# Expert tiles: turning the hidden activations in 32x32 blocks on VectorE and placing them with ScalarE, in place of TensorE's transposes

## The reference, cut to what matters

```python
top_v, top_i = jax.lax.top_k(x @ gate_w, 2)
top_p = jax.nn.softmax(top_v, axis=-1)
combine = zeros((T, 8)).at[arange(T)[:, None], top_i].add(top_p)
g = einsum('th,ehi->tei', x, Wg)           # 256 -> 704
u = einsum('th,ehi->tei', x, Wu)           # 256 -> 704
d = einsum('tei,eih->teh', silu(g) * u, Wd)  # 704 -> 256
expert_out = einsum('te,teh->th', combine, d)
shared = silu(x @ Sg) * (x @ Su) @ Sd
```

## Time and profile before

| what | value |
|---|---|
| median of 3 runs | 1810.65 us (1805.61 to 1811.26) |
| the profiled execution, its time | 1814.42 us |
| the profiled execution, its span | 1812.6 us |
| busy: PE, DVE, ACT, POOL | 1569.5, 1152.0, 854.1, 1046.7 us |
| expert stage, first gate multiplication to last down multiplication | 1183.86 to 1770.90 us |
| granted TensorE clock over the span | 0.945 |

### The profile page before, as it was taken

How to read it: one execution, slowest core, us unless ns; L and a number is a source line. 1 busy time by engine, 2 the same in 40 slices (tenths; PEclk the granted TensorE clock), 3 DMA queues, 4 the chain that set the end, 5 groups by cost and what they waited for, 6 DMA issues and landing times.

```text
span 1812.6 us, 23920 instructions
## 1 busy us (share of the span) xinstructions
PE 1569.5 (87%) x7068; PEld 1057.0 (58%) x7068; DVE 1152.0 (64%) x1928; ACT 854.1 (47%) x1480; POOL 1046.7 (58%) x1233
## 2 busy tenths in 40 slices
PE   5888798898898898898898768699999999999990
PEld 2354555555555655655555645467777777777770
DVE  2299998898898898898898997222222222222225
ACT  3566657657658657658657554222112222121214
POOL 0579779779778779778778885312222222222224
PEclk9899899999999999999999968799999999999995
DMA  3111112211211111111111652514212222222216
GB/s 96 48 35 48 47 47 73 73 48 49 73 45 55 65 46 58 65 42 58 60 48 47 219 157 73 171 42 113 43 33 34 33 33 34 34 34 34 34 28 191
DMA packets 84393, 116.21 MB, mean 64 GB/s; under 512 B 11120, under 2 KB 58576, under 8 KB 84272
## 3 DMA queue, kind: packets, MB, share of 16 engines
q1 hardware_dynamic: 63344, 82.94, 14.6%
q0 software_dynamic: 16704, 27.57, 7.8%
q10 hardware_dynamic: 4224, 4.19, 0.7%
HBM read 81.05 MB, written 33.10 MB: 63 GB/s over the span
## 4 chain that ended last, share of the span: by engine, by line
PE 37%; DVE 5%; issue 4%; POOL 3%; ACT 2%; DMA 1%; DVEq 0%; POOLq 0%; ACTq 0%; SPq 0%
PE A L1255 10%; PE bA L1214 9%; PE bH L1214 9%; DVE arena L862 2%; PE bY L1238 2%; POOL arena L1019 1%; PE bH L592 1%; DVE arena_t L879 1%; DMA sum_scratch<-arena_t 1%; PE A L1246 1%; PE A L522 1%; PE A L1238 1%; PE A L577 1%; PE A L564 1%; PE A L555 1%
## 5 line engine op out<-in xcount | busy, mean ns | idle before, releaser
L1019 POOL TENSOR_TENSOR arena<-arena 128x512 f32<-128x512 f32 x512 | 645.5, 1273 | 175.5 <-DVE arena L862 173.0
L736 ACT ACTIVATE bA<-arena,a_neg 128x512 f32<-128x512 f32 x512 | 353.6, 692 | 284.0 <-DVE arena L862 278.7
L592 PEld LDWEIGHTS bH<-ident,arena 128*128 128x128 f32 x2048 | 260.8, 149 | 316.9 <-issue 147.6
L592 PE MATMUL bH<-ident,arena 128*128 128x128 f32 x2048 | 336.0, 292 | 89.0 <-DVE arena L862 75.5
L862 DVE TENSOR_TENSOR_SCAN arena<-bA,arena 128x512 f32<-128x512 f32 x256 | 305.8, 1209 | 45.0 <-ACT bA L736 32.1
L862 DVE TENSOR_TENSOR_SCAN arena<-bA,hl,arena 128x512 f32<-128x512 f32 x256 | 322.0, 1270 | 13.9 <-ACT bA L736 13.9
L1350 POOL DMA_INDIRECT sum_scratch<-arena_t x71 | 113.5, 1598 | 187.1 <-issue 156.5
L1386 ACT ACTIVATE arena_t<-bA 128x352 f32<-128x352 f32 x142 | 58.1, 461 | 322.3 <-PE bA L1214 322.3
L1255 PE MATMUL A<-arena,hT 128*128 x852 | 195.8, 379 | 0.8 <-ACT hT L1392 0.8
L1344 POOL DMA_DIRECT2D arena_t<-expert_in_scratch x71 | 40.7, 573 | 257.7 <-PE A L1246 208.2
L1214 PE MATMUL bA<-arena,arena_t 128*128 x568 | 179.8, 459 | 1.3 <-ACT arena_t L1397 1.3
(11 more groups left out here) (194 smaller groups left out, 2118.4 us busy)
## 6 DMA issues: line engine op xcount, KB each, us to landing
arena<-b_scratch SPq DMA_DIRECT2D x128, 256.0 KB, 3.2
arena_t<-expert_in_scratch POOLq DMA_DIRECT2D x71, 132.0 KB, 2.4
arena<-in_L_ffn_Wg_dram SPq DMA_DIRECT2D x8, 704.0 KB, 6.0
arena<-in_L_ffn_Wu_dram SPq DMA_DIRECT2D x8, 704.0 KB, 7.1
arena<-in_L_ffn_Wd_dram SPq DMA_DIRECT2D x8, 640.0 KB, 8.2
arena<-in_L_attn_x_dram SPq DMA_DIRECT2D x8, 512.0 KB, 4.9
arena_x<-in_L_attn_x_dram SPq DMA_DIRECT2D x8, 512.0 KB, 5.0
x_scratch<-arena_x SPq DMA_DIRECT2D x8, 512.0 KB, 3.2
```

The costliest lines, as they stand in the source:

```text
L592: i = e.transpose(bH[g % NH][:, q * P:(q + 1) * P], hh[:, (n - 1) % 2, q, d * P:(d + 1) * P], ident[:])
L736: e.activation(bA[g % NA][:], dt[c % 2][:, d, :], ACT.Exp, scale=a_neg[:, d, n:n + 1]).then_inc(s_a, 1)
L1019: e.tensor_tensor(bb[:, k % NB, :], u[c % 2][:, d, :], br[:, n % NR, :], ALU.mult).then_inc(s_bb, 1)
```

## The change

Gone are TensorE's `pe_turn_h` and the copies of its results to `hT` on ACT and DVE. In their place, DVE turns `hm` by one transpose instruction in place (`dve_turn`), which turns every block of 32 tokens by 32 features where it stands and moves none of them. Of the 22 blocks of a group of 32 partitions, blocks q, q+4, q+8, ... belong on partitions 32q to 32q+31 of `hT`, so ACT then copies, for each of 4 targets q and each of 4 token groups a, 32 partitions with 6 blocks (q = 0, 1) or 5 blocks (q = 2, 3) of 32 columns (`act_place`): 16 instructions for a tile. `act_place(t-1)` is the first thing ACT does in a turn of its loop, ahead of silu(t). `pe_down` now waits for these copies alone; the semaphores `s_ka` and `s_kb` are gone, `s_hb` is new, and `s_th` now counts placed tiles.

```diff
-    def pe_turn_h(e, t):
-        e.wait_ge(s_h, t + 1)
-        if t:
-            e.wait_ge(s_ka, t)
-            e.wait_ge(s_kb, t)
-        for q, (i0, n) in enumerate(FIT):
-            b, o = (bHA, q) if q < NB4 else (bHB, q - NB4)
-            i = e.transpose(b[0:n, o * P:(o + 1) * P], hm[:, t % 2, i0:i0 + n], ident[:])
-        i.then_inc(s_th, 1)
-
...
     def pe_down(e, t, ex):
-        e.wait_ge(s_ka, t + 1)
-        e.wait_ge(s_kb, t + 1)
+        e.wait_ge(s_th, t + 1)
...
+    def dve_turn(e, t):
+        e.wait_ge(s_h, t + 1)
+        e.transpose(hm[:, t % 2, :], hm[:, t % 2, :]).then_inc(s_hb, 1)
+
+    def act_place(e, t):
+        e.wait_ge(s_hb, t + 1)
+        if t >= 2:
+            e.wait_ge(s_dn, t - 1)
+        for q in range(P // BLK):
+            n = (FI // BLK - q + P // BLK - 1) // (P // BLK)
+            for a in range(P // BLK):
+                i = e.copy(hT[q * BLK:(q + 1) * BLK, t % 2, 0:n, a * BLK:(a + 1) * BLK],
+                           hm[a * BLK:(a + 1) * BLK, t % 2, :].rearrange("p (b i) -> p b i", i=BLK)[:, q::P // BLK, :])
+        i.then_inc(s_th, 1)
...
@@ def pe_tiles
-            if t:
-                pe_turn_h(e, t - 1)
...
@@ def act_tiles
         for t in range(-1, NT + 1):
+            if t >= 1:
+                act_place(e, t - 1)
             if 0 <= t < NT:
                 e.wait_ge(s_g, t + 1)
...
-            if t >= 1:
-                e.wait_ge(s_th, t)
-                if t >= 3:
-                    e.wait_ge(s_dn, t - 2)
-                e.copy(hT[:, (t - 1) % 2, 0:NB4, :].rearrange("p k q -> p (k q)"), bHA[:]).then_inc(s_ka, 1)
...
@@ def dve_tiles
-            if t:
-                e.wait_ge(s_th, t)
-                if t >= 3:
-                    e.wait_ge(s_dn, t - 2)
-                for q in range(NB4, NF):
-                    n = FIT[q][1]
-                    i = e.tensor_copy(hT[0:n, (t - 1) % 2, q, :], bHB[0:n, (q - NB4) * P:(q - NB4 + 1) * P])
-                i.then_inc(s_kb, 1)
...
                 i.then_inc(s_h, 1)
+                dve_turn(e, t)
```

More of the change, by code:

```diff
@@ L68 @@
 NR = NB = 4
-NF, NB4, NX = len(FIT), 4, 4
+NF, NX, BLK = len(FIT), 4, 32
 UT = 4
@@ L1185, in program @@
     gt = sb("gt", [P, 2])
-    bX, bG, bU, bHA, bHB, bD = A[0], bA, bH, bY, A[1], A[2]
+    bX, bG, bU, bD = A[0], bA, bH, A[2]
     s_wt = sem("s_wt")
@@ L1190, in program @@
     s_tx = sem("s_tx"); s_kx = sem("s_kx"); s_g = sem("s_g"); s_gu = sem("s_gu"); s_si = sem("s_si"); s_h = sem("s_h")
-    s_th = sem("s_th"); s_ka = sem("s_ka"); s_kb = sem("s_kb"); s_dn = sem("s_dn"); s_yt = sem("s_yt"); s_ys = sem("s_ys")
+    s_hb = sem("s_hb"); s_th = sem("s_th"); s_dn = sem("s_dn"); s_yt = sem("s_yt"); s_ys = sem("s_ys")
     acc = arena[:, 0:NU * UT * DM].rearrange("p (u j d) -> p u j d", u=NU, j=UT)
```

## The result

The changed kernel takes 1823.2 us (median of 4 runs, 1822.77 to 1828.72) where the one before takes 1810.76 us in the same series: a ratio of 1.0082, with a 95% interval of 1.0056 to 1.0109. It is slower by 12.4 us, where 44 us less was forecast. The profiled execution took 1828.72 us, with a span of 1826.9.

A forecast was written before the change was run, and what follows sets the result against it. TensorE was taken as the bound of the expert tiles, before and after. Terms of -46.2, +0.3 and +1.9 gave -44.0 us, from 1810.65 to 1766.7 us; 1760 to 1780 had 78%, and 8 in 10 reached to 1788.

The forecast's parts named there:

- what TensorE gains: Expert tiles: six transposes fewer, 0.66 us of TensorE, so a tile takes 7.54 us, not 8.20; 46.2 us over 70.
- the seam: Where up follows gate on TensorE: assumed to close up; 0.1 us lost there would leave 37 us of gain, 1774 us.
- the sum: Whole kernel: -46.2 on TensorE, + 0.3 at the start, + 1.9 at the end = -44.0 us.
- the block transpose: DVE's turn of hm in each tile: 0.93 us, bounded by 0.52 and 1.75.
- the duration of a copy: ACT's copies from hm to hT: 368 ns for 192 columns, 342 ns for 160.
- sixteen copies then take 8 x (0.254 + 0.228) + 0.114 = 3.97 us: ACT's copies of one tile: each overlaps the next by 0.114 us, so all 16 last 3.97 us.
- The loop: Turn, copies, silu, product, back to turn, with three hand-overs: 6.8 us, 0.73 under TensorE's 7.54, so it hides.
- The first rival: Copies don't overlap, ScalarE's loop binds at 8.52 us a tile: 28 us slower, 1839 us; chance 9%.
- The upper bound of the copy term: ACT's 16 copies of a tile without any overlap: 5.68 us.
- Start and end: First tiles lose about 0.3 us once; in the tail the last down comes 2.1 later and 1.9 us are lost.

The follow-up runs named there:

- one copy: The changed kernel with one of a tile's 16 copies, the other 15 left out and hT zeroed once at the start; 1769.17 us in one run.
- one-letter experiment: The changed kernel with copy (q, a) reading partitions 32q to 32q+31 in place of 32a to 32a+31; 1768.93 us, 0.9786 times the kernel before.
- split kernel: The changed kernel with 8 of a tile's 16 copies made by VectorE, the other 8 by ScalarE; 1767.89 us, 0.9769 times the kernel before.
- ScalarE's old order: The changed kernel with ScalarE doing silu of this tile first, then the 16 copies of the tile before, then the xtT copy; 2189.22 us in one run.

## Why the prediction was wrong

- **Right: what TensorE gains.** A tile of 7.54 us was forecast; with one copy it is 7.54, and gate to up is 2.36 or 2.37 in every kernel without transposes between them. The loss of 0.1 us at the seam did not come. Over the 69 tiles from the second gate to the last, though, the kernel with one copy gains 42.6 us and not 69 x 0.66 = 45.5: the eleventh tile loses 5.6 us over its steady length there and 2.8 before, for which the sum had no term. The Trainium skill's 390 ns for a transpose (VectorE: DVE Perf Modes, The three transpose paths), by which 164 us would have gone (an estimate from its figure), was rightly set aside for the trace's 0.11 us.
- **Right: the block transpose.** 0.91 us measured, 0.93 taken from the row of L903 scaled by columns; the bounds were 0.52 and 1.75.
- **Right: the duration of a copy**, nearly: 0.350 and 0.321 us, 0.368 and 0.342 forecast.
- **Wrong: the step "sixteen copies then take 8 x (0.254 + 0.228) + 0.114 = 3.97 us".** They take 5.54. I took the overlap of 0.114 from two instructions of the scan stage that both work on all 128 partitions, and wrote that I saw no reason for 32 partitions to cost more. The number of partitions costs nothing (a copy of 48 columns takes 0.229 us with 32, 64 and 128 of them); that they change from one copy to the next does, and the rows could not show it, because ScalarE's instructions of the kernel before all start at partition 0. All 16 copies lose it, 1.3 us a tile measured by the one-letter experiment.
- **From there the rest follows.** The loop is 8.35 us and not 6.8, over TensorE's 7.54 and over the 8.20 of before. The first rival had this mechanism, its place and its point: from 335 ns a copy on the kernel is slower, and measured are 5.54/16 = 346. Its price, 28 us, was too high against 12.4, or 17.3 in the expert stage alone: a tile is 8.35 us where it had 8.52, since the copies are 0.14 us shorter in all, the turn 0.02, and the hand-overs, of which the loop has four and not three, come to 0.13 and not 0.15. It had 9%. The upper bound of the copy term was on the other side of the loop's threshold, and the only evidence between the bounds was one pair of unlike instructions; that called for more than 9%.
- **Wrong: "Start and end", too low.** From the last gate to the last scaling the tail lost 7.0 us, where the prediction's own times give 1.4 (the last down 2.1 later, less the 0.66 us of the transposes that went from there). Of the 5.6 between them 2.6 are the last down multiplication at half the clock, a term that the prediction did not have; 1.6 are the longer copies; 1.4 are the last silu, late behind the copies before it, so that the last product ends 7.33 us behind the last gate and not 5.94. At the start, the tile behind the second gate takes 9.65 us, 1.3 over the steady tile, where 0.3 stood.

## What to carry to other kernels

Before work is moved off the bounding engine, close the loop that the moved work now lies in (here copies, silu, product, transpose) and ask at which price per instruction it passes the old period; when that price lies between the bounds of an unmeasured term, the sign of the result is open, whatever the likeliest value says. An overlap between neighbouring instructions is a property of the pair: take it only from a pair whose partitions, read and written, follow each other as in the case at hand. Where many small copies stand on one engine's queue ahead of something urgent, share them between two engines; here that alone turned 12 us lost into 40 won.

## What the hardware showed beyond that

- ScalarE's instructions from SBUF to SBUF start about 0.095 us before the one ahead has ended when both read and write the same partitions (128, 64 or 32 of them, also when the 32 read are others than the 32 written), and not at all when the partitions read or those written start elsewhere than the ones before. It held for 48 columns (0.134 apart against 0.24) and, by the experiment with the letter, for 192 and 160. In the kernel before, neighbours whose number of partitions changes (128 to 32, 32 to 128, 128 to 96) while all start at 0 do overlap, by 0.09 to 0.11 us (944.74 + 0.56 = 945.30, next 945.20), so it may be the first partition that counts; those pairs have PSUM on one side, and no probe here changed the number alone. ScalarE's timeline there:

```profile
944.74 0.56 ACT L653 COPY arena<-A 32x512 f32<-32x512 f32 x1
945.20 0.68 ACT L736 ACTIVATE bA<-arena,a_neg 128x512 f32<-128x512 f32 x1
```

- VectorE's 8 copies of 32x160 between groups of partitions last 0.256 us each and take 2.11 us, so they do not overlap either. That it is for the same reason was not tried.
- A VectorE transpose of 704 float32 columns in 32x32 blocks, in place, takes 0.91 us: 1.3 ns a column with its fixed part.
- TensorE's clock fell after 5.49 us of idling (the next multiplication at 0.51), after the 4.74 us at the split kernel's eleventh tile (0.52) and, in the kernel with ScalarE's old order, after 3.99 us (0.61 in the tile shown; the down multiplication takes 4.2 to 5.3 us in others). After the 2.47 us in the split kernel's tail the last down took 2.85 us at a granted clock of 1.00.
